# A two-layer gated cross-attention kernel with routed experts: the second layer's expert tiles given two tables, the first made and used while the last router groups are still chosen

## What is computed

```python
x = x + jnp.tanh(g_xattn[1]) * _L1_xattn_ref(_layernorm(x), ctx_1024, Wq, Wkv)   # 16 heads of 8
x = x + jnp.tanh(g_ffn[1]) * _L1_ffn_ref(_layernorm(x), gate_w, w1, b1, w2, b2)

# _L1_ffn_ref: 8 experts, 128 -> 512 -> 128, each row goes to its best two
probs = softmax(xt @ gate_w.T)
top_w, top_i = top_k(probs, 2);  top_w = top_w / (top_w.sum(-1) + 1e-9)
out = sum over k of top_w[:, k] * (gelu(xt @ w1[top_i] + b1) @ w2[top_i] + b2)
```

## Time and profile before

| what | value |
| --- | --- |
| median of 3 runs | 704.15 us |
| runs | 704.15, 701.25, 704.49 us |
| span of the profiled execution | 703.2 us; its time beyond the span isn't given apart from the runs |
| TensorE, VectorE, ScalarE, POOL busy | 79%, 72%, 51%, 44% |
| second layer's attention | up to about 512 us |
| expert tiles of the second layer | 541.4 to 689.7 us |

### The profile page before, as it was taken

One profiled execution on the slowest core, in us unless ns is written; L12 is line 12 of the kernel. 1 busy time (PEld: TensorE's weight loads), 2 busy tenths in 40 slices (PEclk: granted clock), 3 DMA queues, 4 the chain that ended last, 5 costly groups with the idle time before them and its releaser, 6 DMA issues.

```text
span 703.2 us, 17741 instructions
## 1 busy us (share of the span) xinstructions
PE 554.3 (79%) x5770; PEld 451.8 (64%) x5770; DVE 503.1 (72%) x1617; ACT 359.2 (51%) x860; POOL 307.0 (44%) x431
## 2 busy tenths in 40 slices
PE   6789999998830118997698989898742999999992
PEld 4667677776630007886566766676532899999992
DVE  5988889888358893442699999999745556566652
ACT  2267777776733104451156777676721555555550
POOL 5512233221110017744764215565777555556553
PEclk9899999999975557999889999999975999999997
DMA  5354434532020003342546555543112222343443
GB/s 175 93 146 126 137 108 139 150 110 82 18 76 1 0 8 83 99 88 57 161 128 182 164 169 156 140 123 95 42 38 85 72 73 78 118 137 106 126 134 105
DMA packets 99865, 72.61 MB, mean 103 GB/s; under 512 B 13272, under 2 KB 93272, under 8 KB 99752
## 3 DMA queue, kind: packets, MB, share of 16 engines
q1 hardware_dynamic: 88496, 53.64, 26.3%
q0 software_dynamic: 6816, 14.10, 6.9%
q10 hardware_dynamic: 4464, 3.73, 1.9%
HBM read 42.14 MB, written 29.85 MB: 102 GB/s over the span
## 4 chain that ended last, share of the span: by engine, by line
PE 52%; DVE 24%; issue 9%; ACT 5%; DMA 5%; POOL 3%; SPq 1%; POOLq 0%; ACTq 0%; DVEq 0%
PE bank L1066 14%; PE bank L1056 12%; PE bank L823 7%; DVE MX L1239 6%; PE bank L860 5%; PE bank L991 4%; PE bank L844 4%; DVE PT L1470 2%; DVE XN L1282 2%; PE bank L940 2%; ACT OT L759 2%; ACT XT_HL_WR L735 1%; DMA QS_N<-MH 1%; PE bank L896 1%; PE bank L907 1%
## 5 line engine op out<-in xcount | busy, mean ns | idle before, releaser
L702 ACT ACTIVATE PT<-bank 128x512 f32<-128x512 f32 x256 | 151.8, 598 | 90.7 <-PE bank L844 89.6
L1239 DVE TENSOR_REDUCE MX<-bank 128x4 f32<-128x512 f32 x256 | 172.7, 681 | 19.8 <-PE bank L860 18.0
L860 PE MATMUL bank<-KS,QS_N 96*128 96x128 f16 x1024 | 102.6, 224 | 11.5 <-DVE MX L1239 6.9
L1066 PE MATMUL bank<-WALL,HT 128*128 x780 | 104.6, 281 | 5.0 <-issue 2.0
L662 POOL DMA_INDIRECT returned<-PT,META_ROW x78 | 79.0, 1012 | 66.3 <-DVE PT L1591 50.8
L1066 PEld LDWEIGHTS bank<-WALL,HT 128*128 128x128 f32 x780 | 96.8, 193 | 14.5 <-issue 12.5
L1056 PE MATMUL bank<-XGT,XT_HL_WR 128*128 128x256 f32 (+1 forms) x468 | 100.5, 352 | 0.1
L844 PE MATMUL bank<-QS_N,KS 98*128 98x512 f16 x256 | 96.8, 384 | 2.5 <-DMA QS_N<-MH 2.2
L860 PEld LDWEIGHTS bank<-KS,QS_N 96*128 96x128 f16 x1024 | 76.0, 102 | 34.2 <-DVE MX L1239 12.3
L1056 PEld LDWEIGHTS bank<-XGT,XT_HL_WR 128*128 128x128 f32 x468 | 79.1, 197 | 6.8 <-issue 0.3
L790 ACT ACTIVATE XGT<-bank 128x128 f32<-128x128 f32 (+1 forms) x78 | 25.8, 330 | 106.2 <-PE bank L823 106.2
(11 more groups left out here) (238 smaller groups left out, 945.3 us busy)
## 6 DMA issues: line engine op xcount, KB each, us to landing
spread<-XT_HL_WR SPq DMA_DIRECT2D x96, 128.0 KB, 2.0
QS_N<-spread SPq DMA_DIRECT2D x128, 48.0 KB
KS<-spread SPq DMA_DIRECT2D x32, 192.0 KB
PT<-dispatched SPq DMA_DIRECT2D x39, 132.0 KB, 2.1
WALL<-in_w SPq DMA_DIRECT2D x8, 578.0 KB
CT<-in_ctx SPq DMA_DIRECT2D x32, 128.0 KB, 2.6
returned<-PT SPq DMA_DIRECT2D x39, 64.0 KB
WALL<-in_w ACTq DMA_DIRECT2D x8, 256.0 KB, 2.9
```

The source lines that it names most:

```text
L702: nc.scalar.activation(PT[:, c, 4 * g:4 * g + 4, :].rearrange("p j q -> p (j q)"), ST[i % 2][:, :], ACT.Exp, scale=SCALE[layer]).then_inc( ...
L860: last = nc.tensor.matmul(MB[i % 2][:, j * P:(j + 1) * P], QS[0:96, m.r, J * g + j, c * P:(c + 1) * P], KS[0:96, m.r, g, c * P:(c + 1) * P ...
L1066: last = nc.tensor.matmul(bank[6 + a.u][:, c * D:(c + 1) * D], HT[:, a.u, m, c * P:(c + 1) * P], WALL[:, bass.ds(r + (W1COLS[layer] + m * ...
L1239: V.tensor_reduce(out=MX[:, m.u, 2 * J * g + c:2 * J * (g + 1):2], in_=MB[i % 2][:, :].rearrange("p (j k) -> p j k", j=J), op=ALU.max, axi ...
```

## The change

`GROUPS` becomes 3, 3, 3, 2, 3, 2 pairs. The rows of the first four groups (11 pairs, 5632 rows over 8 experts) fill at least 15 tiles whatever the routing is; these get a table of their own, and the other 24 a second one. Attention now runs slots -4 to 16. What the slots 17 to 20 held, and the choice of groups 4 and 5, moves into functions `drain(i)` that each engine calls at the start of tile slot i. The last pair is 15 (`LAST`), the one before it 14. The first table's keys are made in slot 15, its places and columns in slot 16, the second's in tile slots 6, 7 and 8. Banks 4 and 7 now serve the drain, so the tiles use one bank for their transposes (5, PG) and one for their results (6, PA). The `stay_busy` calls of the slots 17 to 20 go with the slots. The table loses its column for the group. `confirm` and `groups_done` go; each group has a scatter semaphore of its own.

```diff
-GROUPS = ((0, 3), (3, 3), (6, 3), (9, 3), (12, 2), (14, 2))
+GROUPS = ((0, 3), (3, 3), (6, 3), (9, 2), (11, 3), (14, 2))
+EARLY_GROUP = 3
+EARLY = -(-(sum(GROUPS[EARLY_GROUP]) * 4 * P - E * (TILE - 1)) // TILE)
...
-            for p in range(-4, PAIRS + (3, 5)[layer]):
+            for p in range(-4, PAIRS + (3, 1)[layer]):
...
             for i in range(-2, n + 1):
+                if drain:
+                    drain(i)
                 slot(lambda d: Tile(layer, i + d) if 0 <= i + d < n else None)
...
-            return min(sum(CHUNKS[k]) * 2 * P // TILE + E - 1, TILES[1])
+            return min(max(sum(CHUNKS[k]) * 2 * P // TILE + E - 1, EARLY + E), TILES[1])
...
                 sp.wait_ge(pads, 16)
+                sp.wait_ge(av_done, 4 * PAIRS - 1)
                 sp.wait_ge(tables_ready, 2)
+                stored_groups(0, EARLY_GROUP + 1)
                 for i in range(TILES[1]):
+                    if i == EARLY:
+                        sp.wait_ge(tables_ready, 3)
+                        stored_groups(EARLY_GROUP + 1, len(GROUPS))
-                    need = sp.value_load(TBL[0:1, 2, i:i + 1], min_val=1, max_val=len(GROUPS))
-                    sp.wait_ge(groups_done, need)
```

POOL, attention slots and the tile loop:

```diff
+                    older = [(k, b) for k, b in todo if not d or b < d.b]
+                    newer = todo[len(older):]
+                    gated = older[1:] if a else []
+                    for k, b in older[0:1] if a else older:
+                        dispatch(k, b)
...
+                    for unit, (k, b) in zip(range(7 - len(gated), 7), gated):
+                        pool.wait_ge(s_banks, 8 * a.g - 4 + unit + 1)
+                        dispatch(k, b)
+                    if newer:
+                        pool.wait_ge(g_weight, d.k + 1)
+                        for k, b in newer:
                             dispatch(k, b)
                     if z:
+                        deviations(z)
...
+                        ends = ((0, 2, 7, 12), (0, 2, 7, 12), (0, 2, 8, 12), (0, 4, 8, 8))[k]
...
             def second_experts():
-                confirm(Group(len(GROUPS) - 1))
+                deviations(LAST)
+                rest_of_stores(4, 0, 12)
                 for i in range(TILES[1]):
+                    if i in (4, 5):
+                        rest_of_stores(5, 4 * (i - 4), 4 * (i - 3))
```

ScalarE's and TensorE's `drain`, the table's products in the attention slots, and the banks:

```diff
+                if i == -2:
+                    normalise(BEFORE_LAST)
+                    keep_transposed(BEFORE_LAST)
+                if i == -1:
+                    keep_logits(BEFORE_LAST)
+                    shares(Group(4))
+                if i == 0:
+                    normalise(LAST)
+                if i == 1:
+                    keep_transposed(LAST)
+                if i == 2:
+                    keep_logits(LAST)
+                if i == 4:
+                    shares(Group(5))
...
+                    if layer == 1 and p == PAIRS:
+                        table_order(0)
+                        table_rows(0)
...
+                    if layer == 1 and p == PAIRS - 1:
+                        pe.wait_ge(m_split, a.g + 1)
+                        table_counts(0)
...
+                if i == -2:
+                    transposed(BEFORE_LAST)
+                if i == -1:
+                    logits(1, BEFORE_LAST)
+                    pe.wait_ge(g_mask, 5)
+                    pe.wait_ge(o_kept, 2 * PAIRS)
+                    rank_group(Group(4))
+                if i == 1:
+                    transposed(LAST)
+                if i == 2:
+                    logits(1, LAST)
+                if i == 5:
+                    pe.wait_ge(g_mask, 6)
+                    pe.wait_ge(g_read, 5)
+                    rank_group(Group(5))
+                    table_counts(1)
+                if i == 7:
+                    table_order(1)
+                if i == 8:
+                    table_rows(1)
...
-                        pe.wait_ge(xg_kept, before(a.g - 1))
+                        pe.wait_ge(xg_kept, before(a.g - 1 + layer))
-                            last = transpose(bank[4 + a.u][:, c * P:(c + 1) * P], rows[:, c, 0:D])
+                            last = transpose((bank[4 + a.u], PG)[layer][:, c * P:(c + 1) * P], rows[:, c, 0:D])
...
-                        pe.wait_ge(y_kept, before(a.g - 1))
+                        pe.wait_ge(y_kept, before(a.g - 1 + layer))
+                        if layer == 1 and a.i == EARLY:
+                            pe.wait_ge(tables_ready, 3)
```

```diff
+                        if layer == 1 and (p, u) == (PAIRS - 1, 5):
+                            table_keys(0)
+                        if layer == 1 and (p, u) == (PAIRS, 1):
+                            table_places(0)
+                        if layer == 1 and (p, u) == (PAIRS, 3):
+                            table_columns(0)
...
+            def drain(i):
+                if i == -1:
+                    divide(1, LAST)
+                    add_attention(LAST)
+                    second_stats(LAST)
+                    steps(4, range(12))
+                    steps(4, (13, 14, *WEIGHTS))
+                if i == 3:
+                    steps(5, range(7))
+                if i == 4:
+                    steps(5, range(7, 12))
+                if i == 5:
+                    steps(5, (13, 14, *WEIGHTS))
+                if i == 6:
+                    table_keys(1)
+                if i == 7:
+                    table_places(1)
+                if i == 8:
+                    table_columns(1)
...
+                if part == 0:
+                    ts(ex[1], BASE[:, n - 1, :], -float(TILE - 1), ALU.add)
+                    starts(1)
+                else:
+                    link(V.tensor_copy(ex[1], BASE[:, n - 1, :]))
+                    starts(1, TAKEN[:, :])
+                if part == 1:
+                    tt(ex[4], ex[4], TAKEN[:, :], ALU.subtract)
```

More of the change, by code:

```diff
@@ L713, in slot @@
                     if y:
[L714 to L718 removed]
+                        normalise(y)
                     exponentials(b, 7)
@@ L803, in slot @@
                             last.then_inc(gelu_done, 1)
-                tile_slots(layer, slot)
+                tile_slots(layer, slot, None, drain if layer else None)
             for layer in range(2):
@@ L996, in attention_slot, with transposed, logits @@
                 return slot
+            def transposed(y):
+                pe.wait_ge(n_copied, y.g + 1)
+                pe.wait_ge(lg_kept, y.g)
+                for c in range(2):
+                    last = transpose(PF[:, 256 + c * P:256 + (c + 1) * P], N[:, y.b + c, 0:D])
+                last.then_inc(n_t, 1)
+            def logits(layer, y):
+                pe.wait_ge(n_kept, y.g + 1)
+                for c in range(2):
+                    last = nc.tensor.matmul(PF[:, 256 + E * c:256 + E * c + E], NT[:, c * P:(c + 1) * P],
+                                            WG[:, layer, :], start=True, stop=True)
+                last.then_inc(lg_done, 1)
@@ new lines, in rank_group @@
+            def rank_group(d):
+                n = d.n
+                to = PO[:, 0:n * E].rearrange("p (b e) -> p b e", e=E)
+                mask = MASKG[:, d.k, :, :]
+                nc.tensor.matmul(to, BEFORE[:, :], mask[:, 1:n + 1, :], start=True, stop=False)
+                nc.tensor.matmul(to, ONES[:, :], SHARE[:, :].unsqueeze(1).broadcast_to([P, n, E]), start=False, stop=False)
+                for k in range(n):
+                    last = nc.tensor.matmul(to[:, k:, :], ONES[:, :],
+                                            mask[:, k:k + 1, :].broadcast_to([P, n - k, E]), start=False, stop=(k == n - 1))
+                last.then_inc(g_rank, 1)
@@ new lines, in table_rows @@
+            def table_rows(part):
+                pe.wait_ge(order_ready, 2 * part + 2)
+                to = (PG, PF)[part]
+                n = PARTS_OF_TILES[part][1]
+                for k in range(3):
+                    last = nc.tensor.matmul(to[:, 2 * P + k * n:2 * P + (k + 1) * n], VALUES[:, k:k + 1].broadcast_to([P, P]),
+                                            PLACE[:, 0:n], start=True, stop=True)
+                if part == 0:
+                    last = nc.tensor.matmul(to[:, 3 * P:3 * P + E], ONES[:, :], EARLY_MINE[:, :], start=True, stop=True)
+                last.then_inc(ordered, 1)
@@ new lines, in table_columns @@
+            def table_columns(part):
+                first, n = PARTS_OF_TILES[part]
+                these = slice(first, first + n)
+                chain.sync()
+                dve.wait_ge(ordered, part + 1)
+                read = (PG, PF)[part]
+                start, expert, filled = (read[:, 2 * P + k * n:2 * P + (k + 1) * n] for k in range(3))
+                link(V.tensor_copy(FILLED[:, 0, these], filled))
+                link(V.scalar_tensor_tensor(out=STARTF[:, these], in0=start, scalar=float(TILE), in1=FILLED[:, 0, these], op0=ALU.mult, op1=ALU.add))
+                link(V.tensor_copy(TBL[:, 0, these], STARTF[:, these]))
```

(3 more changed lines are left out.)

276 lines of the change are left out of this document (135 added, 141 removed).

## The result

The changed kernel took 710.42 us in the median of 6 runs (708.14 to 711.98), the kernel before beside it 704.77 (701.25 to 706.34, 6 runs): ratio 1.0074, 95% interval 1.0053 to 1.0094. It is slower by some 5 us (0.7%) where 6 us of gain were forecast, and it lies outside the range of 691 to 708. The profiled execution has a span of 708.6 us against 703.2.

A forecast was written before the change was run, and what follows sets the result against it. Bound: TensorE for the 39 expert tiles, and a gap before them. Gain 13.7 - 2.1 (TensorE blocks) - 4.2 (keys and group 5's steps) - 0.6 (sums of chunks) - 0.7 (last product) = 6.1 us: 704.15 to 698.0, range 691 to 708.

The forecast's parts named there:

- The start: Ahead of the tile loop: first product of expert weights at 528.2 instead of 541.9, a gain of 13.7 us (bounds 10 and 17).
- the router's branch: Slots 15 to 17: pair 13's deviations, exponential, group 4's mask at 524.6, ranks, then first transposes; leads to 527.9.
- POOL, SP and the transposes' bank at nothing: In the tile loop: POOL's scatters and SP's queued loads cost nothing; the single transposes bank got no loop cost.
- ScalarE's two table loads at nothing: At tile 4, around group 5's Exp among Gelus: 2.8 us with the Exp, inside 4.2 us of room, so no cost.
- The keys: Second table's keys, 4.9 us of VectorE work in tile slot 6: TensorE waits 3.7 us in slot 7 (bounds 1.5 and 5).
- so the second products of a tile wait for the tile before: 603.55 - 603.08 = 0.47 us is left: Steady tile slots: with one result bank, the hand-over from VectorE's results to TensorE's next second products has 0.47 us left.
- The last product: End of the tile loop: with one bank the last tile's second products wait, costing 0.7 us (bounds 0 and 1.1).
- B: Wait ahead of line 1066: single result bank paces every tile, 0.3 us beyond the margin over 39 tiles, 709.8 us; chance 0.13.
- spacing over 3.8 in steady slots: Sign in the steady tile slots that the single result bank sets the pace; the forecast had 3.73 us.
- C: Tile loop: interruptions cool TensorE to half clock or delay Gelu, costing 5 us, 703 us; chance 0.12.
- D: Start of the tile loop: first fifteen tiles' loads come only after all groups are scattered, 712 us; chance 0.04.
- TensorE's other blocks: Inside the tile loop: pair 15's transposes and logits, group 5's ranks and counts, the table's products, 2.1 us on the path.

The follow-up runs named there:

- experiment 10: All four follow-up edits together on the changed kernel, plus POOL taking pair 13's deviations ahead of slot 15's four new scatters: 694.43 us, 0.9829 to the kernel before.
- experiment 5: The kernel before with one bank instead of two for the gathered rows' transposes, results still in two: 706.61 us, ratio 1.0008.
- experiment 1: The changed kernel with TensorE's weight address read moved ahead of the wait for results: 755.83 us, 0.9913 on the first chip; 697.62 us, 0.9887 on the third.
- 9: The changed kernel with the read first, results freed early, two result banks from tile 8 and the keys spread: 694.19 us, ratio 0.9836 to the kernel before.
- experiment 6: The changed kernel again, unaltered, as control on the second chip: 709.57 us, ratio 1.0059 to the kernel before.
- 7: The changed kernel with TensorE waiting only for the bias addition, the results bank's last reader, read still behind the wait: 699.38 us, ratio 0.9903 to the kernel before.
- experiment 8: The changed kernel with the second table's keys made in four parts in tile slots 6 to 9, later steps moved back: 706.64 us, ratio 1.0002 to the kernel before.
- 4: The kernel before with one result bank and the weight address read ahead of the wait, first chip: 766.46 us, ratio 1.0031.
- experiment 3: The kernel before with one bank for the second layer's results, nothing else changed: 782.46 us, 1.0248 on the first chip; 718.88 us, 1.0196 on the third.

## Why the prediction was wrong, point by point

- **The start: right.** 14.65 us won where 13.7 were forecast. Slot 14 moved its followers by 2.2 us (the transposes of OT from 497.05 to 499.21), forecast 1.9; pair 13's deviations ended at 514.56, forecast 514.7; the last scatter at 519.61, forecast 519.8; group 4's ranks began at 525.28, forecast 524.6 for the mask; the first load at 522.18, forecast 522 to 523.8. In the changed kernel the router's branch is the later one, by some 1.2 us (experiment 10); the forecast had the two within 0.5. The product was put at 528.2 and came at 527.25.
- **POOL, SP and the transposes' bank at nothing: right**, the last by experiment 5; no results or rows are waited for in the steady slots of experiments 1 and 9.
- **ScalarE's two table loads at nothing: right.** Each takes 1.28 us, ready Gelus follow within 0.02 us of the second, and TensorE has no pause at tile 4 that VectorE's wait doesn't explain. The Trainium skill, "ScalarE: Activation LUTs", What ACT_TABLE_LOAD costs, has a switch at about 2.66 us, a load of 1.28 and a drain of 1.38. The trace agrees on the load; it shows no drain, neither as a row nor as a gap, as the first load starts 0.02 us behind the Gelu ahead of it (542.61 for 542.59). The rule of the Trainium skill's section on table sets, to batch calls by table set, broken by this change, would not have bought anything in this kernel, since the loads lie in idle time.
- **The keys: right in mechanism, short in size.** 3.7 us were forecast; 7.66 less 4.05 is 3.6. What was missing is the spacing behind it, 5.57 for 4.05, with half clock in part of it: 1.5 us. They belong to the profiled execution only; in the traces of experiments 1 (third chip), 6 and 7 the block costs as much (7.65, 7.74, 7.66) and the spacing behind it stands at 3.98, 4.07 and 3.95 at the full clock. Spreading the keys gained 2.9 (experiment 8).
- **The step that failed: "so the second products of a tile wait for the tile before: 603.55 - 603.08 = 0.47 us is left".** The 0.47 was there: a bare hand-over, from results kept to the first weights, takes 0.13 us (experiment 1, last tile), so one bank alone fits. But it was read from a kernel in which the wait was already met, so what stood behind the wait, the read of line 1063, had run before. With the wait live, the read is added: 0.91 us from kept to weights, a loop of 4.06 against 3.73, 0.32 us for each tile. Over 37 spacings (29 at the end and 8 ahead of them) that is 11.7 us, nowhere in the sum. Four experiments bear on it alone: moving the read takes the changed kernel to 0.9887 from 1.0059 (experiments 1 and 6) and the kernel before with one bank to 1.0031 from 1.0248 (4 and 3, same chip); one bank with the read behind the wait costs the kernel before 1.0196 (3 again), and a start of the hand-over 0.52 us sooner hides the read (7, 0.9903). With the read moved the kernel takes 697.62 us, next to the 698.0 of the forecast: the other terms held, in sum.
- **The last product, 0.7 (bounds 0 and 1.1): wrong by the same step**, 2.2, as the loop stands bare there: 4.19 us between the last two, where 1.96 stood.
- **The rival that came true was B**, "the single result bank sets the pace of every tile", at "the wait ahead of line 1066", 709.8 us; measured 710.42. Its place was right, with chance 0.13, and its 0.3 us a tile is near the 0.32 measured. That the time agrees within 1 us is in part luck: the 0.3 was a supposition, and the end of the loop (1.5 more than forecast) and the half clock of the profiled execution are balanced by the better start and by the blocks below. What it lacked is the reason: it looked for jitter beyond 0.47 us, where a fixed piece of queued instructions was to be counted, and "Against: the margin is measured in steady slots" fell with it. The stated range of 691 to 708 also left B's own price, 709.8, outside. Its mark, "spacing over 3.8 in steady slots", is what the trace shows.
- **C is part of it only**: half clock for about 3 us behind the keys, in the profiled execution and not in that of experiment 6. D is out: the first load goes out at 522.18, ahead of the second table.

In sum, for the profiled execution: 14.65 won; lost 11.7 to the read behind the wait, 2.2 at the end, 5.1 to the keys' stall and the slot behind it (3.6 + 1.5), the remaining 1.1 to TensorE's other blocks and the first tile. Those blocks had been put at 2.1 us; how much of them the slower pace hides can't be taken apart in the trace of after, since TensorE has idle time there.

## What to carry to other kernels

Before a buffer goes from two to one, write out the loop that closes through it, and count every instruction that stands behind the live wait on its queue, register reads included: a margin read off a trace where the wait was already met says nothing of them. Put address reads ahead of the wait, and signal a bank free at its last reader instead of at the end of the chain that follows. A serial block of 4.9 us of small operations on an engine with 1.8 us free a slot belongs in parts over several slots: here that was worth 2.9 us.

## What was not expected of the hardware

- The read of one table value into a register of TensorE's queue takes 0.47 us (0.30, 0.15 and 0.02) and some 0.6 with the gaps between the three, where a bare hand-over from VectorE's end to the first weight load takes 0.13. It is in no busy time: the weight queue shows 0.43 to 0.46 us of idle time ended by "issue".
- A group of 16 second products takes 2.05 us instead of 1.95 when its first weight load isn't hidden behind other products: weights and matmul then start together (607.90 and 607.91), where they stand 0.21 apart otherwise (605.46 and 605.67).
- The same kernel took 761 us on one chip and 705 to 706 on two others, 8% apart, while the ratios of experiments 1 and 3 agree within 0.3 and 0.5% of each other across two of them. Of the 65.1 us between the spans of experiment 3's two traces (781.0 and 715.9), 59.6 lie ahead of the first tile's second products (604.96 and 545.38). In experiment 1 on the slower chip two of the first six spacings are 13.5 and 14.3 us, where they are 4.1 and 7.7 on the other. What causes either was not looked into.
